# Cross-attention on one core: x and the context also loaded in transposed layout, the on-chip transposes of both taken out

## The reference, cut to what matters

```python
def layer_norm(x, gamma, beta):
    mu = mean(x); var = mean(square(x - mu))
    return (x - mu) * rsqrt(var + 1e-5) * gamma + beta

# x: (64, 256, 512), ctx: (64, 256, 384), all float32
text_p  = x   @ W_text  + b_text          # 512 -> 512
audio_p = ctx @ W_audio + b_audio         # 384 -> 512
Q, K, V = layer_norm(text_p, g1, beta1), layer_norm(audio_p, g2, beta2), audio_p
alpha   = softmax(Q @ K.T / sqrt(512))
out     = layer_norm((alpha @ V) @ W_out + b_out + x, g_out, beta_out)
```

## Time and profile before

| engine | busy us | share of the span | instructions |
|---|---|---|---|
| PE | 1436.8 | 97% | 8240 |
| PEld | 1219.4 | 82% | 8240 |
| DVE | 1147.9 | 77% | 1657 |
| ACT | 855.9 | 58% | 1547 |
| POOL | 1050.5 | 71% | 1223 |

### The profile page before, as it was taken

One profiled execution on the slowest core, in us unless ns is written; L12 is line 12 of the kernel. 1 busy time (PEld: TensorE's weight loads), 2 busy tenths in 40 slices (PEclk: granted clock), 3 DMA queues, 4 the chain that ended last, 5 costly groups with the idle time before them and its releaser, 6 DMA issues.

```text
span 1486.0 us, 26150 instructions
## 1 busy us (share of the span) xinstructions
PE 1436.8 (97%) x8240; PEld 1219.4 (82%) x8240; DVE 1147.9 (77%) x1657; ACT 855.9 (58%) x1547; POOL 1050.5 (71%) x1223
## 2 busy tenths in 40 slices
PE   8999999999999999999999999999999999999996
PEld 6788888888888888888888888888888888888885
DVE  6578777887777887777887778877778877788777
ACT  5465666555665555665556656556655466655563
POOL 2466777667867667776678676677776777766786
PEclk9999999999999999999999999999999999999999
DMA  5212221122221122211222211222212222112211
GB/s 191 71 43 86 100 99 53 67 85 92 99 99 46 66 90 93 99 67 53 85 92 99 99 49 64 92 92 99 84 43 78 92 99 99 51 67 87 93 50 58
DMA packets 63449, 121.44 MB, mean 82 GB/s; under 512 B 8385, under 2 KB 24769, under 8 KB 63425
## 3 DMA queue, kind: packets, MB, share of 16 engines
q1 hardware_dynamic: 63424, 121.14, 22.6%
HBM read 62.40 MB, written 33.55 MB: 65 GB/s over the span
## 4 chain that ended last, share of the span: by engine, by line
PE 33%; DVE 28%; POOL 23%; issue 12%; ACT 2%; DVEq 1%; SPq 1%; POOLq 0%; DMA 0%; ACTq 0%
POOL y_rows L901 8%; DVE qT_lo L663 8%; POOL y_rows L903 5%; DVE y_rows L685 5%; PE wide L255 5%; PE wide L253 5%; PE wide L254 5%; DVE q_cols L657 4%; PE turn L260 4%; DVE y_bn L690 3%; DVE row_max L700 3%; POOL squares L866 2%; DVE cT_lo L613 2%; POOL y_sc L859 2%; PE score L253 2%
## 5 line engine op out<-in xcount | busy, mean ns | idle before, releaser
L253 PE MATMUL wide<-xT_hi,wt_hi 128*128 128x512 f32 x512 | 209.9, 410 | 0.0
L255 PE MATMUL wide<-xT_hi,wt_lo 128*128 128x512 f32 x512 | 202.0, 395 | 0.0
L254 PE MATMUL wide<-xT_lo,wt_hi 128*128 128x512 f32 x512 | 201.9, 394 | 0.0
L895 POOL TENSOR_TENSOR y_rows<-x_in,bao_row 128x512 f32<-128x512 f32 x128 | 176.6, 1401 | 9.5 <-DVE bao_row L738 9.5
L507 ACT ACTIVATE qT_hi<-q_cols,beta_col 128x512 fp32r<-128x512 f32 x128 | 90.6, 725 | 154.7 <-DVE q_cols L657 154.7
L903 POOL TENSOR_TENSOR y_rows<-y_rows,betao_row 128x512 f32<-128x512 f32 x124 | 170.2, 1372 | 9.7
L901 POOL TENSOR_TENSOR y_rows<-y_rows,go_row 128x512 f32<-128x512 f32 x124 | 173.8, 1402 | 0.0
L657 DVE SCALAR_TENSOR_TENSOR k_cols<-k_cols,g_col,turn 128x512 f32<-128x512 f32 x128 | 89.6, 740 | 100.3 <-PE turn L260 100.3
L487 ACT ACTIVATE squares<-wide,btc_col 128x512 f32<-128x512 f32 x128 | 88.2, 689 | 135.4 <-PE wide L255 134.1
L857 POOL TENSOR_SCALAR y_sc<-y_mv 128x1 f32<-128x1 f32 x128 | 24.4, 191 | 192.6 <-DVE y_mv L695 187.2
L253 PE MATMUL wide<-cT_hi,wa_hi 128*128 128x512 f32 x384 | 159.3, 415 | 0.0
(11 more groups left out here) (116 smaller groups left out, 4081.1 us busy)
## 6 DMA issues: line engine op xcount, KB each, us to landing
x_in<-in_x SPq DMA_DIRECT2D x128, 256.0 KB, 4.3
out<-y_rows SPq DMA_DIRECT2D x128, 256.0 KB, 2.0
c_in<-in_ctx SPq DMA_DIRECT2D x32, 768.0 KB, 4.6
c_kept<-c_in SPq DMA_DIRECT2D x32, 768.0 KB, 3.5
q_cols<-in_L_xattn_W_text SPq DMA_DIRECT2D x1, 1024.0 KB, 5.6
y_rows<-in_L_xattn_W_out SPq DMA_DIRECT2D x1, 1024.0 KB, 8.1
k_cols<-in_L_xattn_W_audio SPq DMA_DIRECT2D x1, 768.0 KB, 4.7
bao_row<-in_L_xattn_b_out SPq DMA_DIRECT2D x1, 256.0 KB, 8.3
```

What stands on the lines that cost most here:

```text
L253: nc.tensor.matmul(to, a_hi, b_hi, start=(m == 0), stop=False)
L254: nc.tensor.matmul(to, a_hi, b_lo, start=False, stop=False)
L255: done = nc.tensor.matmul(to, a_lo, b_hi, start=False, stop=(m == n - 1))
L895: nc.gpsimd.tensor_tensor(y_rows[odd][:, t, :], x_in[:, t, :], bao_row[:], ALU.add).then_inc(x_biased, 1)
```

## The change

numpy lays x and ctx out in two forms each: by rows, with the four tiles side by side in a partition (`x_rows`, `c_rows`), and transposed (`xT`, `cT`). The kernel loads `xT_in` and `cT_in` and splits from there; `turn_x` and `turn_c` are gone, 7 groups of four transposes in a step. `c_kept` is loaded from HBM instead of copied from `c_in`. `x_in` is gone: the rows of x are loaded in step i itself, straight into `y_rows[odd]`, and `bias_x` works in place. The output has the tiled layout too, and numpy undoes it.

```diff
 # SP
-                wait_apart(sp, c_loaded, 16 * (i + 1))
-                sp.dma_start(c_kept[:], c_in[:]).then_inc(c_copied, 16)
+                load_c(i)                                  # c_kept <- c_rows[i]
                 if not last:
-                    wait_apart(sp, c_copied, 16 * (i + 1))
-                    wait_apart(sp, cT_done, CT * (i + 1))
-                    load_c(i + 1)
-                    wait_apart(sp, xT_done, DT * (i + 1))
-                    for t in range(T):
-                        wait_apart(sp, x_biased, T * i + t + 1)
-                        load_x(i + 1, t)
+                    wait_apart(sp, cT_split, CT * (i + 1))
+                    load_cT(i + 1)
+                if first:
+                    wait_apart(sp, xT_split, DT)
+                    load_xT(1)
+                    sp.wait_ge(wao_done, CT)
+                elif isinstance(i, int) and i == 1:
+                    sp.wait_ge(bao_done, 1)
+                for t in range(T):
+                    if not isinstance(i, int) or i >= 2:
+                        wait_apart(sp, stored[t], 16 * (i - 1))
+                    load_x(i, odd, t)                      # y_rows[odd][:, t] <- x_rows[i, :, t]
+                if not first and not last:
+                    wait_apart(sp, xT_split, DT * (i + 1))
+                    load_xT(i + 1)
 # PE, step
-                    pe.wait_ge(pT_split, NB * j + 1)
-                turn_x(i, 0)
                 project_k(i, 2)
-                if not first:
-                    pe.wait_ge(pT_split, NB * j + 2)
-                turn_x(i, 1)
-                pe.wait_ge(xT_split, DT * i + 1)
-                turn_x(i, 2)
                 project_k(i, 3)
-                pe.wait_ge(xT_split, DT * i + 2)
-                turn_x(i, 3)
...
-                    turn_c(i + 1, 0)
-                    pe.wait_ge(q_normed, HT * (i + 1))
-                    turn_c(i + 1, 1)
 # ACT, DVE (the same for cT)
-                nc.scalar.copy(xT_hi[:, d, :], turn[d % 2][:]).then_inc(xT_hi_made, 1)
+                nc.scalar.copy(xT_hi[:, d, :], xT_in[:, d, :]).then_inc(xT_hi_made, 1)
-                low(xT_lo[:, d, :], turn[d % 2][:], xT_hi[:, d, :]).then_inc(xT_split, 1)
+                low(xT_lo[:, d, :], xT_in[:, d, :], xT_hi[:, d, :]).then_inc(xT_split, 1)
 # POOL, bias_x
                 if t == 0:
                     pool.wait_ge(x_loaded, 16 * T * (i + 1))
-                wait(pool, stored[t], 16 * (i - 1))
-                nc.gpsimd.tensor_tensor(y_rows[odd][:, t, :], x_in[:, t, :], bao_row[:], ALU.add).then_inc(x_biased, 1)
+                rows = y_rows[odd][:, t, :]
+                nc.gpsimd.tensor_tensor(rows, rows, bao_row[:], ALU.add).then_inc(x_biased, 1)
```

More of the change, by code:

```diff
@@ L76, in cross_attention_kernel @@
         g2_col, beta2_col = sb("g2_col", [P, HT]), sb("beta2_col", [P, HT])
-        x_in, c_in = sb("x_in", [P, T, D]), sb("c_in", [P, T, DC])
+        xT_in, cT_in = sb("xT_in", [P, DT, T * P]), sb("cT_in", [P, CT, T * P])
         c_kept = sb("c_kept", [P, T, DC])
@@ L188, in _, with load_cT, load_xT, load_x @@
         def _(sp):
+            def load_cT(i):
+                sp.dma_start(cT_in[:], cT[i]).then_inc(cT_loaded, 16)
+            def load_xT(i):
+                sp.dma_start(xT_in[:], xT[i]).then_inc(xT_loaded, 16)
             def load_c(i):
-                sp.dma_start(c_in[:], c_v[i]).then_inc(c_loaded, 16)
-            def load_x(i, t):
-                sp.dma_start(x_in[:, t, :], x_v[i, :, t, :]).then_inc(x_loaded, 16)
+                sp.dma_start(c_kept[:], c_rows[i]).then_inc(c_loaded, 16)
+            def load_x(i, odd, t):
+                sp.dma_start(y_rows[odd][:, t, :], x_rows[i, :, t, :]).then_inc(x_loaded, 16)
             sp.dma_start(wa_stage[:, 0:CT, :], w_audio.rearrange("(t p) h -> p t h", p=P)).then_inc(wa_loaded, 16)
-            load_c(0)
+            load_cT(0)
             columns = [(ba_col, b_audio), (bt_col, b_text), (g1_col, g1), (beta1_col, beta1),
@@ L211, in store_y @@
                 wait_apart(sp, y_ready, T * j + t + 1)
-                sp.dma_start(out_v[j, :, t, :], y_rows[odd][:, t, :]).then_inc(stored[t], 16)
+                sp.dma_start(out[j, :, t, :], y_rows[odd][:, t, :]).then_inc(stored[t], 16)
             def step(i, odd, first=False, last=False):
@@ L238, in _ @@
                 sp.wait_ge(last_ready[by], count)
-                sp.dma_start(out_v[N - 1, :, t, :], y_rows[1][:, t, :]).then_inc(stored[t], 16)
+                sp.dma_start(out[N - 1, :, t, :], y_rows[1][:, t, :]).then_inc(stored[t], 16)
             for t in range(T):
@@ L396, in step @@
                 project_q(i, 0)
+                if not first:
+                    pe.wait_ge(pT_split, NB * j + 1)
                 turn_sum(i, turn[0], k_summed, k_sum_turned)
@@ L616, in xT_low @@
                 dve.wait_ge(xT_hi_made, DT * i + d + 1)
[L617 removed]
+                low(xT_lo[:, d, :], xT_in[:, d, :], xT_hi[:, d, :]).then_inc(xT_split, 1)
             def cT_low(i, d):
                 dve.wait_ge(cT_hi_made, CT * i + d + 1)
[L621 to L622 removed]
+                low(cT_lo[:, d, :], cT_in[:, d, :], cT_hi[:, d, :]).then_inc(cT_split, 1)
             def pT_low(j, b):
@@ L972, with rows, columns @@
     from concourse.bass_utils import run_bass_kernel_spmd as _run
+    x = _np.asarray(inputs["x"])
+    ctx = _np.asarray(inputs["ctx_768"])
+    B, L, D = x.shape
+    DC = ctx.shape[2]
+    N, TOK = B // 2, 2 * L
+    T = TOK // P
+    def rows(a):
+        return a.reshape(N, T, P, a.shape[2]).transpose(0, 2, 1, 3)
+    def columns(a):
+        return a.reshape(N, TOK, a.shape[2] // P, P).transpose(0, 3, 2, 1)
+    laid_out = [("x_rows", rows(x)), ("xT", columns(x)), ("c_rows", rows(ctx)), ("cT", columns(ctx))]
     nc = _bacc.Bacc("TRN2", target_bir_lowering=False, num_devices=1)
     arrays, args = {}, []
-    for name in _INS:
-        a = _np.ascontiguousarray(inputs[name])
+    for name, of in laid_out + [(name, inputs[name]) for name in _INS]:
+        a = _np.ascontiguousarray(of)
         arrays[f"in_{name}"] = a
         args.append(nc.dram_tensor(f"in_{name}", a.shape, _mybir.dt.from_np(a.dtype), kind="ExternalInput").ap())
-    out = nc.dram_tensor("out", arrays["in_x"].shape, _mybir.dt.float32, kind="ExternalOutput").ap()
+    out = nc.dram_tensor("out", arrays["in_x_rows"].shape, _mybir.dt.float32, kind="ExternalOutput").ap()
     cross_attention_kernel(nc, *args, out)
     r = _run(nc, [arrays], core_ids=[0])
-    return r.results[0]["out"]
+    y = _np.asarray(r.results[0]["out"])
+    return _np.ascontiguousarray(y.transpose(0, 2, 1, 3).reshape(B, L, D))
```

48 lines of the change are left out of this document (13 added, 35 removed).

## The result

The changed kernel takes 1809.6 us (median of 4 runs, 1808.95 to 1816.9) against 1487.35 us for the kernel before on the same chip: a ratio of 1.2176, 95% interval 1.2154 to 1.2197. It is slower by 322 us, where 243 were forecast, and 4.6 us above the upper end of the range. The profiled execution took 1816.9 us and was the slowest of the four.

The account below looks back on a forecast made before the run. Bound: a ring of waits over PE, DVE and POOL, not PE alone. Step 45.24 + 7.2 + 1.0 = 53.4 us; 30 x 8.2 = 246, less 3.5, on 1486.0 gives 1728.5, plus 1.2: 1730 us, range 1650 to 1805.

Parts of the forecast that it names:

- The ring: Closed chain of waits over PE, DVE and POOL in each loop step, 45.24 us, 0.9 us longer than PE's own work.
- The rows of x: x loads issue behind the store of tile 3, bias_x waits for all four; turn_sum of q 7.2 us late each step.
- The landing: Last tile of x lands at 715.7, 9.33 us behind the issue of c_kept at 706.38; bounds 714.2 and 718.3.
- The "two streams" rival: xT_in load shares the engines with x, pairs cost 0.4 each: 11.4 us a step, 1825 us, 13%; landing past 10.5 us.
- From the landing to `turn_sum`: POOL's bias and squares of q, then DVE's add_square, k_low at 1.2 and sum: 7.45 us from bias_x 0.
- PE has 4.03 us of its own work, which stays.: PE's stretch from turn_sum of q to q_rs, 715.97 to 720.00, taken as unchanged at 4.03 us.
- The signs that I had named: Steps 53 to 54 us, PE busy near 77%, POOL idle some 9 at bias_x; wrong if PE's q-sum waits under 6.
- The middle of the ring: From DVE's norm of q to POOL's scale of tile 2, predicted unchanged at 17.42 us.
- Steps 0 and 1: First two steps, where removed transposes and ctx waits were to save 3.5 us in all, between 0 and 7.
- Splitting from SBUF: DVE's xT_low with both inputs in SBUF slows POOL's finish_y: 3 times 0.34, 1.0 us a step, bounds 0 and 1.6.
- x comes in time: Rival: slack behind bias_x covers the delay of x, only contention of 0 to 1.0 us a step counts: 1484 to 1514, 4%.

Follow-up runs that it names:

- the quartered transposes: Kernel before, with each loop group of four transposes of x and ctx cut to one, the rest left out: 1485.4 us, 0.9986.
- the context's half alone: Kernel before with only the ctx part of the change: cT loaded, c_kept from HBM, turn_c gone, x as before: 1470.5 us, 0.9885.
- the run that took the contention out: Changed kernel with xT_lo from step 1 on made from PSUM banks turn instead of xT_in, values left wrong: 1776.6 us, 1.1949.
- by tiles: Changed kernel with a semaphore per tile of x, tiles 0 and 1 loaded before the stores of tiles 2 and 3, context last: 1592.9 us, 1.0719.
- the last of the chain: Kernel with x loaded and awaited per tile, with xT_lo from step 1 on made from PSUM, values left wrong: 1466.3 us, 0.9859.
- x alone on the queue: Changed kernel with x loaded before the context from step 2; context and xT_in loads held until bias_x 0 is through: 1683.7 us, 1.1317.

## Why the prediction was right or wrong

*The bound.* Right. The ring was the bound and PE was not; the quartered transposes moved the step by nothing. That they are worth nothing in the loop holds.

*The rows of x.* The mechanism was right: POOL waits at `bias_x` for the DMA, 7.20 us in the step shown, the squares of q stand behind it, and `turn_sum` of q gets the delay. The landing was mis-sized: 10.24 us behind the issue of `c_kept`, not 9.33, which is 0.9 us a step or 27 us. The bytes did not flow at the full rate from the start (254 and 289 GB/s between 908 and 912, 399 between 914 and 916). The "two streams" rival had set its point at 10.5 us behind the store's issue; x did land 10.9 us behind it (906.7, by the pair of stores ending at 907.01, to 917.59), yet by the run that held `xT_in` back the rival's reason has some 0.4 us of it. That the measured 1809.6 lies nearer to its 1825 than to my 1730 is luck for it. By the Trainium skill, "DMA: Bandwidth & Descriptors", section "Where 436 GB/s comes from", I had put the landing, as an estimate, at 0.8 us more and the sum at 24 us more. The total agrees with that, but the window of 399 GB/s stands above the 358 of its rule, so it agrees without being its mechanism.

*From the landing to `turn_sum`.* 7.86 us for 7.45: the `kT_lo` beside POOL took 1.75 us, where I had taken 1.2.

*"PE has 4.03 us of its own work, which stays."* **This is the step that failed**, and the largest part of the error: the work stayed, its time did not. Behind 5.14 us of standing still PE got a clock of 0.54, and the stretch took 5.87 us. That is 1.84 us a step, 55 us over thirty, of the 80 us by which the forecast was short. I had even written that PE stands still for the delay, and had not asked what it does to the work behind it. The run with PE kept busy shows this cause: the stretch is 4.03 us again, and 42 us come back, 13 less than the term in one step times thirty; where the rest went was not followed up. The Trainium skill, "TensorE: Matmul & The Clock Gate", section "Part 1: The HAM clock gate (the "warmup" mystery)", says that the array runs throttled by default and that work releases it. The rows agree: 0.12 us between starts ahead of the wait, 0.21 behind it. By that rule the 4.03 us had, as an estimate, an upper bound of twice that, which my range lacked.

*The signs that I had named.* One of those that were to show me wrong came true: PE's wait at the sums of q is 5.14 us in this step and 4.6 by the median over the steps, under the 6. PE is busy for 82% of the span where I had 77%. I had put all of PE's idle time at the sums; in the run 136.3 us of it, 4.5 a step, stand at `xT_lo`, and the lower clock fills another part with longer work. POOL stands still for x 7.2 us and not 9, since it first waits 2.65 us for `k_ssq`.

*The middle of the ring* ran 0.76 us shorter than before. 0.64 of this lie between the first `row_max` and `y_bn` of the last two tiles, where the first `neg_max` was not blocked, as in the context's half alone. I had not counted on it; it hid nearly a quarter of the errors above.

*Steps 0 and 1.* I had them gain 3.5 us, and they lost 3.7; what part of this is x and what part the splits was not taken apart.

*Splitting from SBUF.* On POOL's piece of the ring 13.77 us for 13.74, and by the run that took the contention out 1.1 us a step for 1.0. Right for this kernel, where the wait for x covers the rest. But I had priced POOL's side alone. On DVE's, a split took 1.53 us instead of 0.65, and PE's second wait, 136.3 us, comes from it for two thirds: with the contention taken out 45.6 are left. The Trainium skill, "SBUF — State Buffer", section "Who interferes with whom", has a DVE operation with two inputs in SBUF and GpSimd's reads exclude each other, the later one standing until the first is through. The rows agree: 1528 ns in 128 splits, 683 with one input in PSUM.

*The rivals.* "x comes in time" was given 1484 to 1514 us. When x did come in time, by tiles, the time was 1592.9: its price lacked what the contention costs without its cover, 126.6 us or 4.2 a step, and 2.6 of these are the delay of `k_ssq` that I had called hidden. Its mechanism was wrongly priced by some 80 us, and would have been wrong had it come about.

The sum of the step's errors: +1.00 landing, +0.41 the sums, +1.84 the clock, -0.76 the middle, +0.03 the splits = 2.52 us, 53.42 to 55.94. Taken apart by runs, the 343 us between the changed kernel and the last of the chain (1809.6, 1592.9, 1466.3) are 217 us for x coming late, and 127 for the contention behind that; what the clock costs is within both, since it goes from 0.892 over 0.935 to 0.996 in the profiled runs of the three.

## What to carry to other kernels

When a load moves behind the work that frees its buffer, price the whole way from that work to the next use; if a ring closes over it, the delay is paid in every step. Ask of a predicted wait of PE what clock the work behind it will get, and of an input moved from PSUM to SBUF what runs on POOL at that time, on both engines' sides. Take a change apart before judging it: here one half was worth -1.1%, and the other hid it under +23%.

## What the runs showed of the hardware that was not expected

- Sixteen needless matmuls in a step made the kernel 42 us faster: the stretch of TensorE's work behind them took 4.03 us, where it took 5.87 at a granted clock of 0.54 behind a wait of 5.14 us.
- A DVE `tensor_tensor` of 128x512 with both inputs in SBUF took 0.64 us while POOL stood idle and 1.53 us on average beside POOL's operations; with one input in PSUM, 0.68 us.
- A DVE operation on 128x2 elements, `neg_max`, took 0.17 us beside POOL operations on 128x1 and 1.16 us beside one on 128x512.
- x alone on the queue, 1.05 MB in four loads, took 6.4 us from the first issue to its use, by the median over the run; with 2.6 MB issued behind it, 7.4 us; with 1.5 MB ahead of it, 10.4 us from the first issue of all with 1.05 MB more behind it, and 10.0 us without.
